# First attention of a fused network: exp of half the scores scaled and squared, buffers and orders of three engines changed

## The reference

```
xs   = roll(groupnorm(x), (-4, -4));  windows of 8x8 = 64 tokens, 8 heads of 8 channels
q, k, v = xw @ W.T + b;   qn, kn = q, k over their norms
attn = einsum(qn, kn) * exp(min(logit_scale, log 100)) + bias + mask
attn = softmax(attn);     out = einsum(attn, v) @ Wo.T + bo
x    = x + roll(out, (4, 4))
```

## Time and profile before

| what | us |
|---|---|
| median of 3 runs | 1012.9 (1008.73 to 1015.47) |
| the profiled execution, its time | 1015.97 |
| the profiled execution, its span | 1014.0 |
| around the span | 1.97 |
| PE / DVE / ACT / POOL busy over the span | 855.2 / 830.1 / 697.0 / 604.0 |
| L914, 64 times | 43.7 |
| L1576, 64 times | 37.6 |
| L1584, 64 times | 40.1 |

### The profile page before, as it was taken

One profiled execution on the slowest core, in us unless ns is written; L12 is line 12 of the kernel. 1 busy time (PEld: TensorE's weight loads), 2 busy tenths in 40 slices (PEclk: granted clock), 3 DMA queues, 4 the chain that ended last, 5 costly groups with the idle time before them and its releaser, 6 DMA issues.

```text
span 1014.0 us, 20687 instructions
## 1 busy us (share of the span) xinstructions
PE 855.2 (84%) x6419; PEld 478.1 (47%) x6440; DVE 830.1 (82%) x1720; ACT 697.0 (69%) x1318; POOL 604.0 (60%) x645
## 2 busy tenths in 40 slices
PE   4958888859999998788888987589999999999960
PEld 3433333424445763344355544255555556555640
DVE  7987888878866856687768888589999999999986
ACT  1867777736447556555777664288889999999966
POOL 1952222214787654277504777777777788888880
PEclk9978999979999999599999999599999999999985
DMA  6000000020003210000300000211111111111107
GB/s 246 1 2 2 2 2 2 2 79 0 1 1 114 70 44 0 1 2 1 100 1 14 27 26 26 61 56 47 39 45 41 33 34 35 33 35 36 36 21 250
DMA packets 25807, 39.64 MB, mean 39 GB/s; under 512 B 6436, under 2 KB 14632, under 8 KB 25448
## 3 DMA queue, kind: packets, MB, share of 16 engines
q1 hardware_dynamic: 16616, 28.93, 9.0%
q0 software_dynamic: 9088, 9.39, 2.8%
HBM read 24.83 MB, written 13.47 MB: 38 GB/s over the span
## 4 chain that ended last, share of the span: by engine, by line
PE 43%; DVE 23%; POOL 15%; issue 9%; ACT 7%; DMA 1%; POOLq 0%; SPq 0%; another core or an unknown queue 0%; ACTq 0%; DVEq 0%
PE bank L2495 9%; POOL results L808 6%; PE bank L2468 5%; POOL slots L785 4%; PE bank L2028 3%; DVE KSS L914 3%; POOL stage L767 3%; DVE stage L919 2%; PE bank L1945 2%; PE bank L1981 2%; DVE T L896 2%; PE bank L2045 1%; PE bank L2257 1%; PE bank L2070 1%; PE bank L1939 1%
## 5 line engine op out<-in xcount | busy, mean ns | idle before, releaser
L2495 PE MATMUL bank<-stage,big 128*128 128x512 f16 (+1 forms) x858 | 226.4, 384 | 6.9 <-issue 3.0
L808 POOL DMA_INDIRECT results<-T,small x156 | 177.7, 1139 | 44.3 <-issue 35.6
L785 POOL DMA_INDIRECT slots<-T,index x128 | 127.1, 993 | 79.3 <-DVE index L1347 41.4
L1855 ACT ACTIVATE T<-bank 128x512 f32<-128x512 f32 x234 | 139.5, 596 | 28.8 <-PE bank L2495 21.8
L1837 ACT ACTIVATE stage<-T 128x512 f16<-128x512 f32 x234 | 146.4, 626 | 3.5 <-DVE T L1494 2.1
L1494 DVE TENSOR_TENSOR T<-bank,T 128x512 f32<-128x512 f32 x195 | 133.8, 686 | 12.3 <-ACT T L1855 8.3
L1517 DVE TENSOR_TENSOR T<-T,stage 128x512 f16<-128x512 f32 x170 | 117.4, 690 | 1.2
L2495 PEld LDWEIGHTS bank<-stage,big 128*128 (+1 forms) x858 | 78.1, 101 | 59.1 <-issue 17.2
L692 POOL TENSOR_TENSOR stage<-T,small 128x512 f32<-128x512 f32 x32 | 34.2, 1068 | 99.0 <-PE bank L1945 99.0
L2468 PE MATMUL bank<-l2w,stage 128*128 (+1 forms) x936 | 90.8, 219 | 0.1
L2468 PEld LDWEIGHTS bank<-l2w,T 128*128 128x128 f16 x780 | 53.7, 98 | 69.3 <-issue 46.4
(11 more groups left out here) (395 smaller groups left out, 1970.9 us busy)
## 6 DMA issues: line engine op xcount, KB each, us to landing
stage<-slots SPq DMA_DIRECT2D x39, 130.0 KB, 2.1
stage<-in_w3l SPq DMA_DIRECT2D x8, 373.0 KB, 3.0
stage<-in_w1l SPq DMA_DIRECT2D x8, 320.0 KB, 3.0
results<-T,small POOLq DMA_INDIRECT x156
T<-in_xw SPq DMA_DIRECT2D x4, 512.0 KB, 6.1
X<-in_xi SPq DMA_DIRECT2D x1, 2048.0 KB, 13.4
slots<-T,index POOLq DMA_INDIRECT x128, 2.2
X<-results SPq DMA_DIRECT2D x8, 256.0 KB, 5.5
```

What stands on the lines that cost most here:

```text
L785: pool.indirect_dma_start(slots_d, bass.IndirectOffsetOnAxis(ap=index[:, k, n:n + 1], axis=0), rows5[:, n * RW:(n + 1) * RW], None).then_i ...
L808: pool.indirect_dma_start(results_d, bass.IndirectOffsetOnAxis(ap=IDS[t % 4][:, i:i + 1], axis=0), Y5[t % 2][:, i, :], None).then_inc(S(f" ...
L1855: nc.scalar.activation(S5[q][to], bank[q][r, :], ACT.Silu).then_inc(S("silu5"), 1)
L2495: mm = nc.tensor.matmul(to[0:m, :], big16[:, bass.ds(e * UPW + o, m)], XT[s], start=(v % 2 == 0), stop=(v % 2 == 1))
```

## The change

Scores are no longer read a second time. The exp of half the score stays in SBUF as f32, in one of eight buffers EX (seven in `stage`, one in `spare`). Its sums come from a matmul that reads the upper 16 bits of each f32 as bf16. The sum's bits are turned into the bits of its rough reciprocal (`RV`, an integer multiply-add, again on DVE), the exps are multiplied by it in place on DVE, and ScalarE squares the result in place: (e^(s/2) / sum)^2. A score bank is released by ACT's exp instead of DVE's add. The order of ACT, DVE and PE in an iteration, and how many iterations behind the scores each later step runs, change too. The first two calls of `stage_queries` are written out, with the same effect.

```diff
-LEVEL = -2.0 * float(np.log(2.0)) / 2.0 ** 23, 254.0 * float(np.log(2.0))
+INVERSE = 254.0 * 2.0 ** 23
+HELD = 8
...
+        RV = [spare[:, 512 + 512 * s:1024 + 512 * s] for s in range(2)]
+        EX = [stage[:, 1024 + 512 * s:1536 + 512 * s] for s in range(HELD - 1)] + [spare[:, 1536:2048]]
...
-            def shift_down(b):
+            def invert_level(b):
                 dve.wait_ge(*when("l0_summed", b + 1))
...
                 if b >= 2:
-                    dve.wait_ge(*when("l0_exp", b - 1))
-                nc.vector.tensor_tensor(SC[b % 2], bank[2 * (u % 2) + g][:, :], LV[b % 2], ALU.add) \
-                    .then_inc(S("l0_shifted"), 1)
+                    dve.wait_ge(*when("l0_scaled", b - 1))
+                nc.vector.tensor_scalar(RV[b % 2].bitcast(I32), bank[4][:, :].bitcast(I32), -1.0, INVERSE,
+                                        ALU.mult, ALU.add).then_inc(S("l0_inverse"), 1)
+
+            def scale_down(b):
+                dve.wait_ge(*when("l0_inverse", b + 1))
+                nc.vector.tensor_tensor(EX[b % HELD], EX[b % HELD], RV[b % 2], ALU.mult).then_inc(S("l0_scaled"), 1)
...
             def divide_unit(u):
-                dve.wait_ge(*when("l0_rsum", u + 1))
+                dve.wait_ge(*when("l0_rsum", 2 * u + 2))
...
-            for k in range(1, UNITS + PER + 1):
+            for k in range(1, UNITS + PER + 3):
                 if k <= UNITS:
-                    shift_down(2 * k - 2)
-                if 3 <= k < UNITS + 3:
-                    divide_unit(k - 3)
+                    invert_level(2 * k - 2)
+                    if k >= 2:
+                        scale_down(2 * k - 3)
+                if 4 <= k < UNITS + 4:
+                    divide_unit(k - 4)
                 if k <= UNITS:
-                    shift_down(2 * k - 1)
-                if k % PER == 3 and k >= 7:
-                    add_images(k // PER - 1)
-                if k % PER == 0 and k >= 8:
+                    invert_level(2 * k - 1)
+                    scale_down(2 * k - 2)
+                if k == UNITS:
+                    scale_down(2 * k - 1)
+                if k % PER == 1 and k >= 9:
+                    add_images(k // PER - 2)
+                if k % PER == 2 and k >= 10:
                     image_stats(k // PER - 2)
...
             def exp_half(b):
                 u, g = b // 2, b % 2
                 act.wait_ge(*when("l0_scores", u + 1))
-                if b >= 2:
-                    act.wait_ge(*when("l0_summed", b - 1))
-                nc.scalar.activation(EH[b % 2], bank[2 * (u % 2) + g][:, :], ACT.Exp, scale=0.5) \
+                if u >= 4:
+                    act.wait_ge(*when("l0_pv", u - 3))
+                nc.scalar.activation(EX[b % HELD], bank[2 * (u % 2) + g][:, :], ACT.Exp, scale=0.5) \
                     .then_inc(S("l0_half"), 1)
...
+            def square(b):
+                act.wait_ge(*when("l0_scaled", b + 1))
+                nc.scalar.activation(EX[b % HELD], EX[b % HELD], ACT.Square).then_inc(S("l0_exp"), 1)
...
-            for k in range(UNITS + 2):
-                for g in range(2):
-                    if k < UNITS:
-                        exp_half(2 * k + g)
-                    if 1 <= k <= UNITS:
-                        exp_scores(2 * k - 2 + g)
-                if k >= 2:
-                    invert_sums(k - 2)
+            for k in range(UNITS + 4):
+                if k < UNITS:
+                    exp_half(2 * k)
+                if k >= 4:
+                    invert_sums(k - 4)
+                if 2 <= k < UNITS + 2:
+                    square(2 * k - 4)
+                if k < UNITS:
+                    exp_half(2 * k + 1)
+                if 2 <= k < UNITS + 2:
+                    square(2 * k - 3)
...
             def scores(u):
                 pe.wait_ge(*when("l0_staged", u + 1))
                 if u >= 2:
-                    pe.wait_ge(*when("l0_shifted", 2 * (u - 1)))
+                    pe.wait_ge(*when("l0_half", 2 * (u - 1)))
...
             def sum_halves(b):
                 pe.wait_ge(*when("l0_half", b + 1))
                 if b >= 1:
-                    pe.wait_ge(*when("l0_level", b))
-                nc.tensor.matmul(bank[4][:, :], sum16, EH[b % 2], start=True, stop=True).then_inc(S("l0_summed"), 1)
+                    pe.wait_ge(*when("l0_inverse", b))
+                high = EX[b % HELD].bitcast(BF16).rearrange("p (n v) -> p n v", v=2)[:, :, 1]
+                nc.tensor.matmul(bank[4][:, :], sum16, high, start=True, stop=True).then_inc(S("l0_summed"), 1)
...
-            for k in range(UNITS + 3):
+            for k in range(UNITS + 5):
                 if 1 <= k <= UNITS:
                     sum_halves(2 * k - 2)
                 if k < UNITS:
                     scores(k)
                 if 1 <= k <= UNITS:
                     sum_halves(2 * k - 1)
-                if 2 <= k < UNITS + 2:
-                    weigh(k - 2)
-                if k % PER == 2 and k >= 6:
-                    project_out(k // PER - 1)
+                if 3 <= k < UNITS + 3:
+                    weigh(k - 3)
+                if k % PER == 0 and k >= 8:
+                    project_out(k // PER - 2)
```

More of the change, by code:

```diff
@@ L247, in network @@
         QX = [stage[:, s * 512:(s + 1) * 512] for s in range(2)]
-        SC = [stage[:, 1024 + s * 512:1536 + s * 512] for s in range(2)]
-        PX = [stage[:, 2048 + s * 512:2560 + s * 512] for s in range(4)]
         PROD = [stage[:, s * 512:(s + 1) * 512] for s in range(6)]
@@ L255, in network @@
         RS = [spare[:, 256 * s:256 * s + 256] for s in range(2)]
-        EH = [spare[:, 512 + 256 * s:768 + 256 * s].bitcast(BF16) for s in range(2)]
-        LV = [spare[:, 1024 + 512 * s:1536 + 512 * s] for s in range(2)]
+        RV = [spare[:, 512 + 512 * s:1024 + 512 * s] for s in range(2)]
+        EX = [stage[:, 1024 + 512 * s:1536 + 512 * s] for s in range(HELD - 1)] + [spare[:, 1536:2048]]
         both16 = rows[:, 0, 0:64].bitcast(F16)
@@ L698, in _ @@
             pool.wait_ge(*when("hmask", 2))
-            for u in range(UNITS):
+            stage_queries(0)
+            stage_queries(1)
+            for u in range(2, UNITS):
                 stage_queries(u)
@@ L909, in _ @@
             runs = [(0, 0, SS, WS), (1, 0, SS + WS, WS - SS), (1, WS - SS, 0, SS)]
-            def shift_down(b):
-                u, g = b // 2, b % 2
+            def invert_level(b):
                 dve.wait_ge(*when("l0_summed", b + 1))
-                nc.vector.tensor_scalar(LV[b % 2], bank[4][:, :].bitcast(I32), LEVEL[0], LEVEL[1],
-                                        ALU.mult, ALU.add).then_inc(S("l0_level"), 1)
-                dve.wait_ge(*when("l0_level", b + 1))
                 if b >= 2:
-                    dve.wait_ge(*when("l0_exp", b - 1))
-                nc.vector.tensor_tensor(SC[b % 2], bank[2 * (u % 2) + g][:, :], LV[b % 2], ALU.add) \
-                    .then_inc(S("l0_shifted"), 1)
+                    dve.wait_ge(*when("l0_scaled", b - 1))
[4 more added lines that the diff above has]
+                nc.vector.tensor_tensor(EX[b % HELD], EX[b % HELD], RV[b % 2], ALU.mult).then_inc(S("l0_scaled"), 1)
             def divide_unit(u):
-                dve.wait_ge(*when("l0_rsum", u + 1))
+                dve.wait_ge(*when("l0_rsum", 2 * u + 2))
                 nc.vector.tensor_tensor(T34[:, 256 * u:256 * u + 256], bank[5 + u % 2][:, 0:256], RS[u % 2],
@@ L1589, in invert_sums @@
                     act.wait_ge(*when("l0_out", u - 1))
-                nc.scalar.activation(RS[u % 2], bank[5 + u % 2][:, 256:512], ACT.Ln).then_inc(S("l0_lnsum"), 1)
-                act.wait_ge(*when("l0_lnsum", u + 1))
+                nc.scalar.activation(RS[u % 2], bank[5 + u % 2][:, 256:512], ACT.Ln).then_inc(S("l0_rsum"), 1)
+                act.wait_ge(*when("l0_rsum", 2 * u + 1))
                 nc.scalar.activation(RS[u % 2], RS[u % 2], ACT.Exp, scale=-1.0).then_inc(S("l0_rsum"), 1)
@@ L1961, in weigh @@
                 to = bank[5 + u % 2]
-                parts = [PX[(2 * u + g // 2) % 4].rearrange("p (j x n) -> p j x n", j=2, x=2)[:, :, g % 2, :]
+                parts = [EX[(2 * u + g // 2) % HELD].rearrange("p (j x n) -> p j x n", j=2, x=2)[:, :, g % 2, :]
                          for g in range(HP)]
```

## The result

The changed kernel takes 1025.25 us, the median of 4 runs (1024.12 to 1027.96), against 1011.34 (1008.73 to 1015.47, 4 runs) for the kernel before: ratio 1.0119 with a 95% interval of [1.0087, 1.015] (the quotient of the two medians is 1.0138). It is slower, as forecast, since the whole interval lies above 1. The prediction's limit of 1% lies inside the interval, so whether it is slower by more than 1% stays open. The profiled execution took 1024.6 us, its span is 1022.8 us.

The account below looks back on a forecast made before the run. The prediction took a ring of waits, no full engine, as the bound. +13.0 between units 4 and 31, -1.4 fill and 0 tail made +11.6: 1027.6 us profiled, 1024.5 against the median; range 1018 to 1036, opened below to 1014.

Parts of the forecast that it names:

- limit of 1%: Slowdown over 1% (10.1 us), about what a measurement can tell: chance 0.64; within 1% 0.30; faster 0.06.
- The ring: Waits from sum_halves through scores, first exp, Ln, Exp, divide and second inverse back to sum_halves: 4.39 us a unit.
- nine links: Inverse to sums 0.15, then 0.21, 0.52, 1.16, 0.49, 0.40, 0.45, 0.33 and the inverse's 0.68 us.
- `project_out`: On TensorE it adds 1.82 us, making the next sum_halves 0.51 late in six iterations: 3.1 us.
- The collision: VectorE's scaling behind add_images meets POOL's query staging: divide 0.13 to 0.42 us late, six times, 1.6 us taken.
- The sum: Units 4 to 31: 27 x 4.39 = 118.5, + 3.1 + 1.6 = 123.2 us against 110.2, so +13.0.
- Fill and drain: Stage's start: units 2, 3 and 4 lose 0.48 us each, -1.4; its end, one iteration deeper: 11.7 against 11.0, +0.7.
- The clock's gain: The last project_out may find TensorE at the higher clock, 1.98 instead of 3.45 us: down to -1.5.
- the tail: The stage's end, deeper drain against a possibly higher clock: taken as 0 us, between -0.8 and +0.7.
- Strided sums and the scaling: Sums reading every second 16-bit value: 0 taken, at most 0.21 us a unit; scaling costed as the replaced add, 0.69.
- Three rivals: No change, 4.0 us a unit: 1014 (0.05); every scaling meets POOL: 1033 (0.08); TensorE's clock lower: 1036 (0.07).
- The faster rival: The divide never waits, so a chunk falls to the engines' own work, about 14.3 of 16.4 us: 999; chance 0.06.

Follow-up runs that it names:

- e1: Changed kernel with ScalarE's inversion of the sums of unit k-4 moved ahead of the first exp of iteration k: 1007.4 us, 0.9953 of the kernel before.
- e7: e1 with the nine image adds spread over three iterations and the statistics in the fourth: 997.72 us, 0.9873 of the kernel before.
- e2: Changed kernel with VectorE's divide of unit k-4 moved behind the second inverse and the scaling of iteration k: 1010.79 us, 0.9981 of the kernel before.
- e5: Changed kernel with add_images moved behind the first scaling of the next iteration: 1025.63 us in a single run.

## Why the prediction was right

- *The ring.* Forecast 4.39, measured 4.43 from the same nine links, none off by more than 0.01. It was shown from four sides: opened on ACT, opened on DVE, put into the kernel before, and lengthened by 0.45.
- *`project_out`.* Forecast +0.51 in six iterations, measured +0.50 (127.58 + 0.68 + 0.15 = 128.41 against 128.91).
- *The collision.* Forecast 1.6 in all, measured six units 0.25 longer, 1.5. Five of them follow the adds, not six: behind the last adds of an iteration with new scores POOL has no unit left to stage. The sixth lies beside the statistics (scaling 1.41 at 158.69), which the forecast did not have. The price was the middle of two, and neither was right: line 896's median excess of 0.56 is too little (the scaling grew by 0.85), and held until POOL's end the divide would be 0.42 late (it was 0.26). So the total is close partly by luck. The rows in which the scaling starts 0.06 behind POOL support the rule in the Trainium skill (SBUF — State Buffer, Who interferes with whom), by which the shared ports are an exclusive lock and the first to start has them for its whole instruction: POOL still had 0.98 us and the scaling grew by 0.85. The last section has the missing 0.13.
- *The sum.* 27 x 4.43 + 6 x 0.50 + 6 x 0.25 = 124.1, as the scores show; forecast 123.2. The nine links, each read 0.01 or less too short, make 1.1 over 27 rings.
- *Fill and drain.* Units 0 to 4 take 16.22 us against 17.42, -1.2 (forecast -1.4): the steps to units 2, 3 and 4 are 0.30, 0.50 and 0.42 shorter, where the forecast had 0.48 each. TensorE's granted clock was 0.50 for most of it in both executions, until 85.5 before and 84.1 after. From the last scores to the last `project_out` 11.98 (forecast 11.7; 11.01 before). The clock's gain, which the forecast counted by half (the tail as 0, between -0.8 and +0.7), came in full in this execution: from the start of the last `project_out` to the adds 2.09 instead of 3.56 us, -1.5. That is luck as far as the runs tell (last section). Together the stage changes by 13.9 - 1.2 + 1.0 - 1.5 = +12.2, where the forecast had +11.6. The near agreement of the totals owes something to misses that cancel: the ring was 1.1 too short, the tail 0.5 too dear.
- *Strided sums and the scaling.* Costed at nothing more than their forerunners: the sums last 0.39 (0.38 to 0.39 before), the next matmuls follow after 0.22 (0.21), the median scaling takes 0.68 against 0.69 for the add. That no cost is hidden under the ring is shown by e1 and e7, where plain units fall to 3.12.

Three rivals fell on the rows: the plain units stand at 4.43, not at 4.0; the granted clock is 0.99 over 82 to 196 us; and 58 of the 64 scalings last under 0.80, so not every one meets POOL. The faster rival (the divide never waits) is what e1 and e2 made, and there its size was wrong: the forecast let the chunk fall to the engines' own work, 14.3 us, and put the kernel at 999. With the ring open the image work no longer hides, and the chunk stays at 16.33. The expectations of e1 and e2 repeated that step. It took the spreading as well (e7, 14.61 us a chunk) to get there.

## What to carry to other kernels

Before moving an instruction in one engine's order, walk the ring that it closes through the other engines, link by link, with starts of one unit of the trace; here the sum of nine such links gave the pace within 1%, while the busy times of the engines barely changed. An early release of a buffer is worth its wait only when no longer ring takes over, so look for the pair of program orders that closes the ring and turn one of them. And when a ring opens, first price the work that hid in its waits: here the image work took back 10.2 of 12.9 us between units 4 and 31 (97.3 with it spread, 107.5 without, 110.2 before).

## What was not expected of the hardware

The hold between VectorE and POOL goes both ways. In the kernel after POOL's staging started 0.18 behind a scaling:

```profile
121.39 0.68 DVE L921 TENSOR_TENSOR stage<-stage,KSS 128x512 f32<-128x512 f32 x1
...
121.57 1.40 POOL L691 TENSOR_TENSOR stage<-T,small 128x512 f32<-128x512 f32 x1 [3.65 <-PE bank L1951]
```

It lasted 1.40 instead of 1.04: 0.36 longer, of 0.50 that the scaling had left. Set beside other meetings in the traces, in us (a scaling alone lasts 0.68, a staging 1.04):

| second to start | what the first had left | longer by |
|---|---|---|
| scaling at 135.41 (kernel after) | 0.98 | 0.85 |
| scaling at 158.69 (kernel after) | 0.86 | 0.73 |
| scaling at 109.84 (e2) | 0.61 | 0.48 |
| scaling at 124.95 (e1) | 0.24 | 0.11 |
| staging at 121.57 (kernel after) | 0.50 | 0.36 |
| staging at 126.34 (e7) | 0.12 | 0.00 |

The second to start pays what the first has left, less a constant 0.12 to 0.14 us, and not a share of it. It looks as if its first 0.13 us needed nothing that the first holds; no run here takes that apart.

The last `project_out` found TensorE at a granted clock of 1.00 instead of 0.50. In the kernel before the clock fell at 208.3, behind five microseconds in which TensorE was busy 1.99:

```profile
203.30:208.30 5.00, 1.99 (x34) 0.79 (x26) 4.90 (x17) 2.72 (x7) 0.00 (x0) 1.00 0.01 3
```

The kernel after, in its drain, shows no fall:

```profile
215.00:220.00 5.00, 3.02 (x36) 1.27 (x29) 4.74 (x9) 4.28 (x11) 0.00 (x0) 1.00 0.00 0
```

So in this execution the higher clock gave back 1.5 us, more than the 1.0 that the longer drain cost. The drain does not ensure it. In e5 TensorE's drain starts at the same distances (from the last scores to the `weigh` ahead of the last but one `project_out` 5.39 us in both), yet the clock fell at 218.8, that `project_out` lasted 2.73 us instead of 1.98, and from the last scores to the last `project_out` passed 13.59 us instead of 11.98:

```profile
220.72 2.73 PE L1988 MATMUL bank<-T,big 128*128 128x512 f32 x4
```

What decided between the two is not shown by any run here.
